# State-space stage: the causal convolution folded into four sets of projection weights, delta times x written over delta, 11 of 32 products with C on GpSimd

## What is computed

```python
xz = x @ W_in.T                                  # x is layer-normed and residual in the kernel
xc, z = split(xz, 2)
xc = silu(causal_depthwise_conv(xc, conv_w) + conv_b)        # 4 taps per channel
delta, Bm, Cm = split(xc @ W_x.T)
delta = softplus(delta @ W_dt.T + b_dt)
deltaA = exp(delta[..., None] * A)
BX = delta[..., None] * Bm[:, :, None, :] * xc[..., None]
hs = scan over time of (h = deltaA * h + BX)
y = einsum('bldn,bln->bld', hs, Cm) + Dp * xc
out = y * silu(z) @ W_out.T
```

## Time and profile before

| | |
|---|---|
| runs | 2048.30, 2059.85, 2059.57 us; median 2059.57 us |
| the profiled execution's own time | 2060.13 us, of it 2058.1 us span |
| first `input_quad` starts | 55.09 us |
| last scan and product of the stage end | 978.0 us |
| stage's output stored, next stage starts | about 994 us |
| mean granted TensorE clock | 0.748 |
| busy over the whole span | PE 59%, DVE 69%, ACT 44%, POOL 56% |

### The profile page before, as it was taken

The page is one execution under the profiler, slowest core; times in us unless marked ns, Lnnn a source line. Parts: engine busy times, 40 slices in busy tenths (PEclk is TensorE's granted clock), DMA queues, the critical chain, the costliest instruction groups (busy, mean ns, idle before and its releaser), DMA issues. The chain is left out here.

```text
span 2058.1 us, 33648 instructions
## 1 busy us (share of the span) xinstructions
PE 1215.0 (59%) x13780; PEld 574.7 (28%) x13780; DVE 1420.7 (69%) x1729; ACT 914.0 (44%) x1665; POOL 1145.3 (56%) x543
## 2 busy tenths in 40 slices
PE   4365646556564646544576636577767775637655
PEld 1112212121211212110232223244445453423322
DVE  3799999999999999899631123776678666536112
ACT  5566564756566564743212214454446443213220
POOL 1889999899999999899300011332443244340100
PEclk8676868676776868665778876787878886768978
DMA  4828182653828182550789960113221322148997
GB/s 123 194 53 197 36 197 72 151 126 84 194 53 197 33 198 65 145 132 0 240 314 379 393 209 18 45 33 74 64 43 51 66 54 64 43 121 355 368 395 287
DMA packets 195624, 301.87 MB, mean 147 GB/s; under 512 B 84176, under 2 KB 126672, under 8 KB 179088
## 3 DMA queue, kind: packets, MB, share of 16 engines
q1 hardware_dynamic: 190656, 297.26, 49.1%
q0 software_dynamic: 2304, 2.37, 0.5%
q10 hardware_dynamic: 2512, 0.10, 0.1%
HBM read 257.21 MB, written 42.47 MB: 146 GB/s over the span
## 5 line engine op out<-in xcount | busy, mean ns | idle before, releaser
L361 POOL TENSOR_TENSOR state<-dx_rep,b_rep 128x2048 f32<-128x2048 f32 x128 | 578.9, 4530 | 64.0 <-PE psum L729 31.7
L472 ACT ACTIVATE psum<-delta_rep,a_neg 128x511 f32<-128x511 f32 x512 | 331.5, 684 | 79.8 <-DVE state L591 79.7
L729 PE MATMUL psum<-state,sel 128*32 128x512 f32 x1024 | 190.5, 834 | 291.2 <-POOL state L370 291.1
L591 DVE TENSOR_TENSOR_SCAN psum<-psum,state 128x1024 f32<-128x1024 f32 x144 | 328.7, 2283 | 33.7 <-POOL state L361 19.9
L591 DVE TENSOR_TENSOR_SCAN state<-psum,state 128x1024 f32<-128x1024 f32 x112 | 255.3, 2279 | 19.9 <-ACT psum L472 19.9
L370 POOL TENSOR_TENSOR state<-state,c_rep 128x1024 f32<-128x1024 f32 x112 | 263.7, 2355 | 0.0
L660 PE MATMUL psum<-xt,w_in 128*128 128x512 f32 x256 | 157.4, 772 | 57.4 <-ACT z_silu L431 26.0
L598 DVE TENSOR_TENSOR state<-psum,c_rep 128x1024 f32<-128x1024 f32 x144 | 176.3, 1224 | 4.9
L856 POOL DMA_DIRECT2D moe_b<-in_w x64 | 33.0, 522 | 258.3 <-DVE moe_xt L1007 257.7
L729 PEld LDWEIGHTS psum<-state,sel 128*32 128x32 f32 x1024 | 27.2, 126 | 421.8 <-issue 374.7
L469 ACT COPY psum<-zeros 128x2 f32<-128x2 f32 x144 | 23.6, 164 | 257.9 <-DVE state L598 253.2
(11 more groups left out here) (214 smaller groups left out, 2503.7 us busy)
## 6 DMA issues: line engine op xcount, KB each, us to landing
moe_w_set<-in_w SPq DMA_DIRECT2D x32, 4096.0 KB, 36.0
delta_rep<-delta_scratch SPq DMA_DIRECT2D x128, 256.0 KB, 5.5
dx_rep<-dx_scratch SPq DMA_DIRECT2D x128, 256.0 KB, 8.2
b_rep<-bc_scratch SPq DMA_DIRECT2D x32, 256.0 KB, 4.8
delta_scratch<-delta SPq DMA_DIRECT2D x32, 256.0 KB, 7.8
dx_scratch<-delta_x SPq DMA_DIRECT2D x32, 256.0 KB, 5.7
c_rep<-bc_scratch SPq DMA_DIRECT2D x32, 256.0 KB, 7.8
moe_x<-x_after SPq DMA_DIRECT2D x16, 512.0 KB, 11.8
```

The costliest lines, as they stand in the source:

```text
L361: nc.gpsimd.tensor_tensor(ring[q % RING][:, :, :], dx_rep[u % CHUNKS][:, :, :], free_bcast(b_rep[q // QPB % 2][:, g, :], 1, CB), ALU.mult) ...
L472: ins = nc.scalar.activation(dec[:, i, 1:], delta_rep[u % CHUNKS][:, c, 1:], ACT.Exp, scale=a_neg[:, dt * CB + c, g:g + 1])
L591: nc.vector.tensor_tensor_scan(bx if by_pool(k) else flat, flat, bx, 0.0, ALU.mult, ALU.add).then_inc(S["scan_done"], 1)
L729: ins = nc.tensor.matmul(bank[32 * c:32 * c + 32, :], sel[:, :], ring[q % RING][:, c, :], start=False, stop=(g == NG4 - 1), skip_group_che ...
```

## The change

The convolution along time is linear, so it can be done with the projection: `project_x` multiplies by four weight sets, one per tap, and reads x shifted by one column each time; eight matmuls a tile accumulate in one bank. The four sets (`w_conv`) are made on the chip at the start: the x half of `W_in` is loaded in rows, transposed back by TensorE (`weights_by_tap`), multiplied by diagonal matrices of the taps (VectorE makes 16 of them, TensorE does 8 matmuls in `weights_scaled`), and copied out of PSUM by ScalarE and VectorE. `taps` and `last_tap` are gone; ScalarE adds the bias in `conv_bias`, one activation a tile, behind halves 10, 12, 14 and 16. `project_x` stands behind quads 1, 2, 3 and 4, one tile each. `delta_x` writes over `delta`, and so waits until delta itself is stored. `by_pool` gives GpSimd the product of 11 halves in 32 instead of 14.

```diff
     def by_pool(k):
-        return k % 2 == 1 and (k // 2) % 8 != 7
+        return k % 2 == 1 and (k // 2) % 16 not in (3, 6, 9, 12, 15)
...
                 def delta_x(b, t):
                     pool.wait_ge(S["delta_ready"], DT * b + t + 1)
                     pool.wait_ge(S["xc_ready"], DT + b)
-                    if b:
-                        pool.wait_ge(S[f"d_stored{t}"], 32 * b)
-                    nc.gpsimd.tensor_tensor(dx[:, t, :], delta[:, t, :], xc[b % 2][:, t, :], ALU.mult).then_inc(
+                    pool.wait_ge(S[f"d_stored{t}"], 32 * b + 16)
+                    nc.gpsimd.tensor_tensor(delta[:, t, :], delta[:, t, :], xc[b % 2][:, t, :], ALU.mult).then_inc(
                         S["dx_ready"], 1)
...
-                def last_tap(b, t):
+                def conv_bias(b, t):
                     act.wait_ge(S["xp_psum"], DT * b + t + 1)
-                    if b == 0 and t >= 2:
-                        act.wait_ge(S["conv_done"], t - 1)
-                    bank = xbank(b, t)
-                    nc.scalar.copy(xpad[t % 2][:, KC - 1:], bank[:, :])
-                    nc.scalar.activation(bank[:, :], bank[:, :], ACT.Identity, bias=conv_b[:, t:t + 1],
-                                         scale=conv_w[:, t, KC - 1:KC]).then_inc(S["xp_read"], 1)
+                    if b >= 2:
+                        act.wait_ge(S["y_gated"], DT * (b - 1))
+                    nc.scalar.activation(xc[b % 2][:, t, :], xbank(b, t)[:, :], ACT.Identity,
+                                         bias=conv_b[:, t:t + 1]).then_inc(S["conv_done"], 1)
...
-                        if i == 10:
-                            last_tap(n, 0)
-                            last_tap(n, 1)
-                        if i == 14:
-                            last_tap(n, 2)
-                            last_tap(n, 3)
+                        if i in (10, 12, 14, 16):
+                            conv_bias(n, i // 2 - 5)
...
-                        if i == 10:
-                            taps(n, (0, 1))
-                        if i == 14:
-                            taps(n, (2, 3))
...
+                def weights_scaled():
+                    for t in range(DT):
+                        pe.wait_ge(S["w_cols"], t // 2 + 1)
+                        pe.wait_ge(S["conv_diag"], t + 1)
+                        if t >= 2:
+                            pe.wait_ge(S["w_conv_act"], t - 1)
+                            pe.wait_ge(S["w_conv_dve"], t - 1)
+                        for k in range(KD):
+                            nc.tensor.matmul(banks[4 + (KD * t + k) % 4][:, :], w_x_cols[:, t, k * P:(k + 1) * P],
+                                             conv_diag[:, t, :, :].rearrange("p k c -> p (k c)"),
+                                             start=True, stop=True).then_inc(S["w_conv_psum"], 1)
...
-                    project(t, xbank(b, t), S["xp_psum"])
+                    bank = xbank(b, t)
+                    for j in range(KC):
+                        for k in range(KD):
+                            ins = nc.tensor.matmul(bank[:, :], w_conv[:, k, j, t * P:(t + 1) * P], xt[:, k, j:j + L],
+                                                   start=(j == 0 and k == 0), stop=(j == KC - 1 and k == KD - 1))
+                    ins.then_inc(S["xp_psum"], 1)
...
-                        if i == 2:
-                            project_x(n, 0)
-                            project_x(n, 1)
-                        if i == 4:
-                            project_x(n, 2)
-                            project_x(n, 3)
+                        if i in (2, 3, 4, 5):
+                            project_x(n, i - 2)
```

More of the change, by code:

```diff
@@ L200, in mamba_phase @@
         nmr = m.sb("neg_mean_rstd", P, ST)
-        xt = m.sb("xt", P, KD, L)
-        xpad = [m.sb(f"xpad{i}", P, KC - 1 + L) for i in range(2)]
+        xt = m.sb("xt", P, KD, KC - 1 + L)
         zs = [m.sb(f"z_silu{i}", P, DT, L) for i in range(2)]
@@ L373, in _ @@
                 nc.gpsimd.memset(zeros[:, :], 0.0).then_inc(S["pads_zero"], 1)
-                for i in range(2):
-                    nc.gpsimd.memset(xpad[i][:, 0:KC - 1], 0.0).then_inc(S["pads_zero"], 1)
+                nc.gpsimd.memset(xt[:, :, 0:KC - 1], 0.0).then_inc(S["pads_zero"], 1)
                 for t in range(DT):
@@ L478, in _ @@
                 norm_apply(0)
+                for i in range(2):
+                    act.wait_ge(S["w_turned"], 2 * i + 2)
+                    nc.scalar.copy(w_x_cols[:, 2 * i:2 * i + 2, :].rearrange("p t n -> p (t n)"), ybank[i][:, :]).then_inc(
+                        S["w_cols"], 1)
                 xt_copies(0)
-                act.wait_ge(S["pads_zero"], 3)
+                for t in range(DT):
+                    act.wait_ge(S["w_conv_psum"], KD * t + 1)
+                    nc.scalar.copy(w_conv[:, 0, :, t * P:(t + 1) * P], banks[4 + KD * t % 4][:, :].rearrange(
+                        "i (k c) -> i k c", c=P)).then_inc(S["w_conv_act"], 1)
+                act.wait_ge(S["pads_zero"], 2)
                 act.wait_ge(S["conv_loaded"], 16 * 2)
                 for t in range(DT):
-                    last_tap(0, t)
+                    conv_bias(0, t)
                 conv_silu(0)
@@ L549, in norm_shift @@
                                                    ALU.mult).then_inc(S["ln_shift"], 1)
-                def taps(b, pair):
-                    for k in range(KC - 1):
-                        for i, t in enumerate(pair):
-                            if k == 0:
-                                dve.wait_ge(S["xp_read"], DT * b + t + 1)
-                            else:
-                                dve.wait_ge(S["conv_step"], 2 * DT * b + 2 * pair[0] + len(pair) * (k - 1) + i + 1)
-                            bank = xbank(b, t)[:, :]
-                            out = bank if k < KC - 2 else xc[b % 2][:, t, :]
-                            nc.vector.scalar_tensor_tensor(out, xpad[t % 2][:, k:k + L], conv_w[:, t, k:k + 1], bank,
-                                                           ALU.mult, ALU.add).then_inc(
-                                S["conv_step"] if k < KC - 2 else S["conv_done"], 1)
                 def softplus_sum(b, t):
@@ L679, in project_z @@
                         pe.wait_ge(S["z_read"], 2)
-                    project(DT + t, mbank[ZBANK[t]], S["z_psum"])
+                    for k in range(KD):
+                        ins = nc.tensor.matmul(mbank[ZBANK[t]][:, :], w_z[:, k, t * P:(t + 1) * P], xt[:, k, KC - 1:],
+                                               start=(k == 0), stop=(k == KD - 1))
+                    ins.then_inc(S["z_psum"], 1)
                 def project_dbc(b):
```

52 lines of the change are left out of this document (36 added, 16 removed).

## The result

| | before | changed |
|---|---|---|
| median of the runs | 2055.39 us (4 runs, 2048.30 to 2059.85) | 2169.79 us (4 runs, 2167.73 to 2177.75) |
| ratio, 95% interval | | 1.0555 (1.0529 to 1.0580) |
| span of the profiled execution | 2058.1 us | 2167.5 us |
| first `input_quad` starts | 55.09 | 109.08 |
| first sequence | 118.6 | 114.8 |

The kernel became 5.6% slower; the forecast was 2156 us in a range of 2095 to 2200. The stage ends 108.5 us later, and these pieces give it: +54.0 at the start, -3.8 in the first sequence, 6 x 10.0 in the middle, -1.8 in the last.

The account below looks back on a forecast made before the run. VectorE and GpSimd were taken as nearly full, in three coupled lists with little slack. Start +27.4 and +28.1, loop +43, first and last sequences -2 and -1 sum to +95.5 on 2060.1: 2156 us, range 2095 to 2200.

Parts of the forecast that it names:

- The start, projections: Before the first sequence: weight making and 32 matmuls instead of 8 delay `project_dbc` from 26.91 to 54.3 us, +27.4.
- The start, stores: Before the first input: products with x wait for delta's stores, some behind chunk loads in the issue order; +28.1 us.
- The loop: TensorE's tiles delay ScalarE's biases and decays, so VectorE scans half 19 43.6 us after `add_output`; sequences take 123.0 us.
- the two clock levels: TensorE's tile of eight matmuls: 7.34 us at 2.4 GHz, 13.3 at 1.2 GHz; the working took 7.34.
- The rest of a sequence: VectorE from half 19 to the next `add_output`: 77.4 us of its 105.3 us work, plus 2 us of waits.
- short waits: VectorE's waits for decays in the rest of a sequence: 2 us added, from 13.8 us over 8 sequences.
- the first and last sequences: The first has no output projection before its tiles, the last has no tiles; the walk gave -2 and -1 us.
- The wait hidden on GpSimd: At a sequence's end `delta_x` waits for delta's stores: +3.4 us on GpSimd, hidden because 110.6 is under 123.0.
- That TensorE's matmuls are hidden: Rival: ring slack and TensorE's idle 49 us swallow the extra matmuls, GpSimd's 110.6 us bounds a sequence; 2075 us, chance 0.14.
- the slow clock: Rival: the full clock is not granted during tiles, 13.3 us each, +24 us a sequence; about 2350 us, chance 0.06.
- the start was not cheaper: Rival of a cheaper start, stores landing early or weights made sooner, loop partly absorbed: 2095 to 2125 us, chance 0.10.

Follow-up runs that it names:

- a_port: The changed kernel with the layer norm's shift made by ScalarE in five small activations instead of by VectorE; ratio to before 1.0482, 122.75 us a sequence.
- the two shortened kernels: The changed kernel with two, and with six, matmuls for a tile of the x projection in place of eight; 2071.80 us and 2125.14 us.
- a_px2: The changed kernel with two matmuls for a tile of the x projection in place of eight, three taps left out; 2071.80 us.
- a_stores: The changed kernel with all four stores of delta issued ahead of the first chunk's loads; 2149.28 us.
- a_pool14: The changed kernel with the old split of the products, 14 of 32 on GpSimd; ratio to before 1.0444.
- b_16: The kernel before with GpSimd taking 16 of 32 products in place of 14; ratio to before 1.0141.

## Why the prediction was right, point by point

**The start, projections: +27.4 predicted, 24.2 measured** (the store of delta 0 goes out at 62.41 instead of 38.22). TensorE in the changed kernel:

```profile
12.53 7.98 PE L668 MATMUL psum<-state 128*128 128x512 f32 x16
21.45 27.71 PE L682 MATMUL psum<-xt,w_conv 128*128 128x512 f32 x64 [0.94 <-issue]
51.97 5.34 PE L705 MATMUL psum<-x_conv,w_x 128*96 128x512 f32 x8 [2.81 <-ACT x_conv L426]
```

The walk was right in its steps: 22.2 for the first tile was 21.45, 54.3 for `project_dbc` was 51.97. A tile takes 6.93, not 7.34: four tiles 1.7 less. The clock was granted at 1.00 from 21.5 to 49.0 us, and `project_dbc`, 6.20 in the earlier trace rows at a granted clock of 0.58, ran in 5.34 at 0.68.

**The start, stores: +28.1 predicted, 29.8 measured** (54.0 less 24.2); 29.0 in the kernel before with this edit alone. The step that held: stores 2 and 3, needed only by late chunks until then, gate the first input. GpSimd in the changed kernel:

```profile
67.56 1.26 POOL L353 TENSOR_TENSOR delta<-delta,x_conv 128x512 f32<-128x512 f32 x1 [65.37 <-DMA delta_scratch<-delta]
87.94 1.26 POOL L353 TENSOR_TENSOR delta<-delta,x_conv 128x512 f32<-128x512 f32 x1 [19.12 <-DMA delta_scratch<-delta]
103.71 1.26 POOL L353 TENSOR_TENSOR delta<-delta,x_conv 128x512 f32<-128x512 f32 x1 [14.50 <-DMA delta_scratch<-delta]
107.86 1.26 POOL L353 TENSOR_TENSOR delta<-delta,x_conv 128x512 f32<-128x512 f32 x1 [2.90 <-DMA delta_scratch<-delta]
```

Two stores behind loads keep it for 19.1 and 14.5 us, one that is alone for 2.9. The two misses cancel: 109.08 against 110.6.

**The loop: 43.6 us from `add_output` to half 19 predicted, 44.1 measured** (263.05 to 307.19 in the second sequence). Its two halves fit too: the last bias began 34.0 us after `add_output` ended (33.5 in the working), and half 19 another 10.0 us later (10.1). TensorE there:

```profile
263.27 8.80 PE L682 MATMUL psum<-xt,w_conv 128*128 128x512 f32 x16 [3.11 <-DVE x_res L574]
272.01 1.06 PE L745 MATMUL psum<-state,sel 128*32 128x512 f32 x8
273.00 7.14 PE L682 MATMUL psum<-xt,w_conv 128*128 128x512 f32 x16
...
281.07 7.14 PE L682 MATMUL psum<-xt,w_conv 128*128 128x512 f32 x16
```

ScalarE, whose decays stand behind its biases:

```profile
272.12 0.69 ACT L419 ACTIVATE x_conv<-psum,conv_b 128x512 f32<-128x512 f32 x1 [10.93 <-PE psum L682]
...
280.18 0.69 ACT L419 ACTIVATE x_conv<-psum,conv_b 128x512 f32<-128x512 f32 x1 [4.88 <-PE psum L682]
...
297.16 0.69 ACT L419 ACTIVATE x_conv<-psum,conv_b 128x512 f32<-128x512 f32 x1 [5.64 <-PE psum L682]
```

And VectorE, which waits for these decays at halves 11, 17 and 19, and for 1.3 us more at halves 13 and 15, 14.2 us in all:

```profile
261.87 1.26 DVE L574 TENSOR_TENSOR x_res<-x_res,psum 128x512 f32<-128x512 f32 x2
...
274.02 2.29 DVE L584 TENSOR_TENSOR_SCAN state<-psum,state 128x1024 f32<-128x1024 f32 x1 [7.43 <-ACT psum L474]
...
299.07 2.29 DVE L584 TENSOR_TENSOR_SCAN state<-psum,state 128x1024 f32<-128x1024 f32 x1 [3.09 <-ACT psum L474]
...
307.19 2.30 DVE L584 TENSOR_TENSOR_SCAN psum<-psum,state 128x1024 f32<-128x1024 f32 x1 [2.38 <-ACT psum L474]
```

Three tiles took 7.14 each, 0.2 less than 7.34; the first took 8.80. The prediction had bounded a tile by the two clock levels and took the full one. For the first tile that was half wrong: TensorE had stood for 3.11 us, and the next rows give the clock before the tile, at its start and after (the column behind the engines).

```profile
260.00:263.20 3.20, 0.17 (x4) 0.00 (x0) 3.20 (x4) 1.19 (x2) 3.20 (x2) 1.00 0.47 88
263.20:267.00 3.80, 3.73 (x5) 1.65 (x6) 3.36 (x2) 0.00 (x0) 3.54 (x1) 0.55 0.41 138
267.00:272.00 5.00, 5.00 (x12) 1.89 (x10) 0.00 (x0) 0.00 (x0) 0.00 (x0) 1.00 0.01 3
```

The first five records ran near the 1.2 GHz level, the rest at 2.4 GHz: +1.7 us on one tile of four. In the last four sequences that have tiles TensorE had stood for 4.7 to 5.2 us, and the first tile took 9.5: +2.3.

**The rest of a sequence: 79.4 us predicted, 81.8 measured.** Here a step failed. The working took VectorE's work as 105.3 us, from the earlier trace rows less the taps and plus the turned halves, with the norm shift in it as it was. That shift, 1.2 to 1.9 us a sequence before (1.5 in the stretch of the earlier trace rows), became 4.48. In the second sequence VectorE was busy 80.4 us in this part, where the working had 77.4: the 3 us are the norm shift's growth. The 2 us for short waits hardly came, 0.34 and little gaps; the working had read them from the V halves' group alone and left out the 19.9 us for which the P halves' scans waited. In a_port, which takes the norm shift off VectorE, a sequence is 122.75, against the 123.0 of the working. So the 2.9 us by which 125.9 exceeds 123.0 are about what this instruction costs; over six sequences 17 us, more than the 13.6 by which the sum was short of the profiled execution's 2169.2. What was left over at the start (-1.5) and in the first and last sequences (-2.6) went the other way.

**The wait hidden on GpSimd.** It was priced at 3.4 and called hidden unless the loop is gone. Alone in the kernel before it costs 3.2 a sequence; in the changed kernel the row in that experiment shows 9.13 us of waiting, and the first scan that reads the input of 348.43 begins at 357.22, 4.3 us after that input is done. No run gives `delta_x` its own tile back in the changed kernel, so that the wait costs nothing there is read from the trace alone.

**The rivals.** That TensorE's matmuls are hidden is refuted by the two shortened kernels. Its 2075 us is near what a_px2 gave (2071.8), but partly by luck: its sequences are 113.5 us, not 110.6, and its start is 19.1 us shorter, which the rival's was not. The clock stayed up but for the first tile's start, so the slow clock's 2350 us is out; the start was not cheaper (54.0 us of 55.5).

**What the change's parts are worth**, from the runs: the stores 20.5 us at the least (a_stores), the tiles' extra matmuls about 98 of the total with their share of the start (a_px2), the split and the norm shift together 26 (a_pool14). They overlap and don't add up to 114. The 12 taps a sequence that VectorE was spared had stood behind halves 10 and 14, inside the part of the sequence in which it now waits for decays; that sparing them brought nothing is argued from there, no run puts them back.

## What to carry to other kernels

Moving work to an engine that is half idle is free only where its idle time lies beside the work it delays: find the engine that waits in list order for each new piece (here ScalarE's bias, with all decays behind it) and walk once round the loop. A buffer saved by writing in place turns a store that nobody waited for into one that gates the next load; where the store must be, issue it ahead of bulk loads. And when a term is taken over from the trace as a duration, ask whether that duration was work or waiting.

## What was not expected of the hardware

A VectorE instruction with both inputs in SBUF (`neg_mean_rstd`, 128x4, 0.16 us when GpSimd is idle) was held up beside GpSimd's float32 instructions. In the changed kernel it begins behind the last scan's product and ends with GpSimd's instruction under way:

```profile
332.37 4.48 DVE L554 SCALAR_TENSOR_TENSOR neg_mean_rstd<-mean_var,rstd 128x4 f32<-128x4 f32 x1
```

```profile
332.32 4.50 POOL L364 TENSOR_TENSOR state<-dx_rep,b_rep 128x2048 f32<-128x2048 f32 x1
```

GpSimd's starts 0.05 us earlier, and both end within 0.03 us of each other. The scans and products, which have one input in PSUM, kept 2.28 and 1.22 us beside GpSimd throughout. In a_pool14 the same instruction took 0.14 to 0.17 us in six sequences; in the second of them it began at 327.66, 0.08 us before GpSimd's next instruction. With 16 of 32 products on GpSimd the wait goes over several of its instructions. VectorE and then GpSimd, second sequence of b_16 (L361 the input, L370 the product with C, L350 delta times x):

```profile
270.13 11.29 DVE L548 SCALAR_TENSOR_TENSOR neg_mean_rstd<-mean_var,rstd 128x4 f32<-128x4 f32 x1
```

```profile
269.85 2.37 POOL L370 TENSOR_TENSOR state<-state,c_rep 128x1024 f32<-128x1024 f32 x1
272.14 2.52 POOL L350 TENSOR_TENSOR delta_x<-delta,x_conv 128x512 f32<-128x512 f32 x2
274.60 4.52 POOL L361 TENSOR_TENSOR state<-dx_rep,b_rep 128x2048 f32<-128x2048 f32 x1
279.05 2.36 POOL L370 TENSOR_TENSOR state<-state,c_rep 128x1024 f32<-128x1024 f32 x1
285.57 2.50 POOL L350 TENSOR_TENSOR delta_x<-delta,x_conv 128x512 f32<-128x512 f32 x2 [4.16 <-DVE delta L566]
```

Five GpSimd instructions followed each other without a gap and VectorE was let in at 281.42, when GpSimd itself had to wait, for VectorE. In other sequences a wait ended between two of GpSimd's instructions, so why it is one or the other is open.

The Trainium skill, page "SBUF — State Buffer", section "SBUF: two separate sides", says that the ports which VectorE and GpSimd share are an exclusive lock, given for one whole instruction to whichever starts first, and that a VectorE operation with two SBUF inputs needs them. The 4.48 us agree. The 11.29 us are longer than one instruction of GpSimd, so here the measurement goes beyond the page.
